# A mixture-of-experts tile loop on VectorE: where the next expert's number is loaded into a register

## The chip, the cores and the metric

The kernel runs on one core of a Trainium2 chip. The metric is the device time of one execution in microseconds. TensorE (PE) multiplies matrices and transposes, ScalarE (ACT), VectorE (DVE) and GpSimd (POOL) compute elementwise, and SyncE (SP) only starts DMAs. Each engine has a sequencer of its own that works through its instructions in order; engines wait for each other through semaphores.

## The reference, cut to what matters

One transformer block over 2048 tokens of width 128, with adaptive layer norm in front of both halves:

```
h = layernorm(x) * (1 + ca) + sa
x = x + ga * attention(h)                     # 16 heads of 64, causal
h = layernorm(x) * (1 + cb) + sb
expert = argmax(h @ Wr.T + br)                # one of 8 experts for each token
y = relu(h @ W1[expert].T + b1[expert]) @ W2[expert].T + b2[expert]
x = x + gb * y
```

The change touches only the last two lines.

## The kernel before, in words

The attention half fills the first 955 us or so. Its order of work on TensorE, ScalarE and VectorE is written out ahead by a planner (`Plan`); the change doesn't touch it.

Then the tokens are sorted by expert. Every token's row is scattered by GpSimd to a place in a table in HBM (`x_sorted`, L557), so that each block of 128 rows belongs to one expert. There are 23 such blocks (`SLOTS`), called tiles below, numbered from 0. `tile_expert` holds in SBUF, as integers, which expert each tile has. All experts' weights lie in SBUF (`experts`), and the four next tiles' own copies of them in `chosen` (`CHOSEN` is 4 places, tile k uses place k % 4). VectorE fills a place by loading the tile's expert number from `tile_expert` into a register (`value_load`, L1067) and copying 1156 columns from an address made with that register (L1068).

For each tile k the engines do this:

- SyncE reads the tile's rows from the sorted table (L525), up to 12 tiles ahead.
- VectorE normalises tile k + 4 (L1086, four tiles ahead: `NORMED` is 4).
- TensorE transposes the normalised tile k + 1 (L724), multiplies tile k with its first weights (`hidden`, L733) and tile k - 2 with its second weights (`output`, L743), in that order. fp32 makes eight matmul instructions of each of the latter two.
- ScalarE scales the transposed tile (L831) and applies bias and relu (L840, four instructions).
- VectorE adds the second bias to the tile's input rows (L1094), waits until TensorE has the tile's result (`y_full`, L1096), for the store of the tile four before (`y_stored`) and for its own sum (L1099), and adds both (L1100), which raises `y_taken`. It waits for `y_taken` (L1104) and copies the weights for tile k + 4 over those of tile k.
- GpSimd waits for `y_taken` and stores the tile's rows to their tokens' places with an indirect DMA (L564).

So TensorE iteration m begins with the transpose of tile m + 1, which needs VectorE's L1086 of tile m + 1, and ends with the result of tile m - 2. VectorE's own order for a tile is L1086, L1094, L1100, L1067, L1068. The copies are made in the tiles 0 to 18; the last four tiles make none. Four copies are made ahead of the loop.

Of the kernel before, what the change touches and what calls it, by code (L numbers as in the profile page):

```python
# [64 lines left out]
class Plan:  # L65
# [8 lines left out]
    def __init__(self):  # L74
# [22 lines left out]
        while any(self.ahead.values()):  # L97
# [4 lines left out]
            if kind is None:  # L102
# [12 lines left out]
                 dve=("norm", "sum", "lo", "add", "resid", "top", "take"))  # L115
# [143 lines left out]

def adaln_block(nc, x, w_qkv, w_out, Wr, br, W1, b1, W2, b2, c_in, wmod, out):  # L260
    _, S, E = x.shape
    _, H, D3 = w_qkv.shape
    D = D3 // 3
    NE, FF, _ = W1.shape
# [7 lines left out]
    SLOTS = T + NE - 1  # L272
    CHOSEN = 4
# [9 lines left out]
    with ExitStack() as ctx:  # L283
        def sb(name, shape, dt=F32):
            return ctx.enter_context(nc.sbuf_tensor(name, shape, dt))
# [85 lines left out]
        tile_expert = sb("tile_expert", [P, SLOTS], I32)  # L371
# [479 lines left out]
        def _(dve):  # L851
# [211 lines left out]
            dve.wait_ge(w2_in, 32)  # L1063
            dve.wait_ge(chosen_known, 1)

            def copy_expert(i, slot_no):
                expert = dve.value_load(tile_expert[0:1, bass.ds(i, 1)], min_val=0, max_val=NE - 1)  # L1067
                dve.tensor_copy(chosen[:, slot_no:slot_no + 1, :],  # L1068
                                experts[:, bass.ds(expert, 1), :]).then_inc(expert_copied, 1)

# [4 lines left out]
                    m = dve.tensor_tensor(w, w, gate_b[:].unsqueeze(1).broadcast_to([P, n, E]), ALU.mult)  # L1075
            link(m)
            for i in range(CHOSEN):
                copy_expert(i, i)

            def normalise_tile(k):  # L1080
                if k >= NORMED:

                    dve.wait_ge(tile_turned, k - NORMED + 1)
                dve.wait_ge(tile_read[k % IN_SLOTS], 16 * (k // IN_SLOTS) + 16)
                row = tile_in[:, k % IN_SLOTS, :]
                dve.tensor_scalar(tile_normal[:, k % NORMED, :], row[:, 0:E], row[:, MEAN:MEAN + 1],  # L1086
                                  row[:, RSTD:RSTD + 1], ALU.subtract, ALU.mult).then_inc(tile_normed, 1)
# [3 lines left out]
            for k in range(SLOTS):  # L1091
                if k + NORMED < SLOTS:
                    normalise_tile(k + NORMED)
                dve.tensor_tensor(tile_x[:, k % 2, :], tile_in[:, k % IN_SLOTS, 0:E],  # L1094
                                  chosen[:, k % CHOSEN, 2 * FF + FT:EXPERT], ALU.add).then_inc(x_summed, 1)
                dve.wait_ge(y_full, k + 1)  # L1096
                if k >= 4:
                    dve.wait_ge(y_stored[k % 4], 16 * (k // 4))
                dve.wait_ge(x_summed, k + 1)  # L1099
                dve.tensor_tensor(tile_y[:, k % 4, :], ps_five[:, 2 + k % 2, 0:E], tile_x[:, k % 2, :],  # L1100
                                  ALU.add).then_inc(y_taken, 1)
                if k + CHOSEN < SLOTS:

                    dve.wait_ge(y_taken, k + 1)  # L1104
                    copy_expert(k + CHOSEN, k % CHOSEN)


# [25 lines left out]
```

## Time and profile before

| | |
|---|---|
| median of 3 runs | 1067.04 us (1066.79 to 1068.41) |
| the profiled execution | 1067.29 us |
| its span from first to last instruction | 1065.5 us |
| PE busy | 999.7 us, 94% |
| DVE busy | 701.0 us, 66% |
| ACT busy | 718.6 us, 67% |
| POOL busy | 43.1 us, 4% |
| granted TensorE clock, mean | 0.98 |

The execution takes 1.8 us more than the span of its instructions. Shares are averages over attention and the tile loop, which have different limits. Names in the rows are those of the buffers in which tiles were placed: `accT` is the normalised tile (L1086) and the biased input (L1094), `v_sb` the finished tile (L1100) and the transposed one (L831), `probs` holds `experts` and `chosen`, `oT` the hidden layer, `hT` the rows as read. DVEq is VectorE's sequencer: instructions there, such as a register load, don't occupy the engine's arithmetic.

### The profile page before, as it was taken

The page shows a single profiled execution, that of the slowest core. Times are in us where ns is not written, and L with a number is a line of the kernel's source. Part 1 is how long each engine was busy: PE and PEld are TensorE (multiplying, and loading weights), DVE is VectorE, ACT ScalarE, POOL GpSimd, SP SyncE. Part 2 cuts the span into 40 slices and gives each one's busy share as a digit, 9 for nine tenths or more (in the row PEclk, how much of TensorE's full clock was granted, in tenths as well). Part 3 has the DMA queues.
Part 4 walks back from the last instruction along what each step waited for, and adds up shares of the span by engine and source line. Part 5 has one row for each costly group of instructions (what it writes and reads, how often), then busy time and mean ns, then how long its engine had stood idle before and what let it go on. Part 6 is the DMA issues. An engine that isn't in the chain of part 4 may idle for free.

```text
span 1065.5 us, 19784 instructions
## 1 busy us (share of the span) xinstructions
PE 999.7 (94%) x7275; PEld 762.3 (72%) x7275; DVE 701.0 (66%) x2234; ACT 718.6 (67%) x1317; POOL 43.1 (4%) x55
## 2 busy tenths in 40 slices
PE   4999999999999999999999999999999999986386
PEld 2677777777777777777777777777777777755376
DVE  4976667856866577666785686657766678555264
ACT  2977767767667677776776776767777677642264
POOL 0000000000000000000000000000000000002444
PEclk9999999999999999999999999999999999996699
DMA  9300020002100020002000210002000100030210
GB/s 202 70 21 1 22 50 21 2 10 48 34 1 2 20 51 21 1 21 50 22 1 19 47 26 1 2 20 51 21 2 21 41 21 1 2 99 16 59 50 17
DMA packets 33199, 31.53 MB, mean 30 GB/s; under 512 B 12181, under 2 KB 22209, under 8 KB 33104
## 3 DMA queue, kind: packets, MB, share of 16 engines
q1 hardware_dynamic: 31856, 28.15, 11.3%
q0 software_dynamic: 1248, 2.13, 0.6%
q8 instruction: 58, 0.95, 0.4%
q14 instruction: 37, 0.30, 0.1%
HBM read 9.83 MB, written 4.12 MB: 13 GB/s over the span
## 4 chain that ended last, share of the span: by engine, by line
PE 85%; DVE 5%; issue 3%; POOL 2%; ACT 1%; DMA 1%; DVEq 1%; SPq 0%; POOLq 0%
PE ps L619 25%; PE ps L656 24%; PE ps L630 22%; PE ps L598 5%; PE ps L639 3%; PE ps L667 3%; PE ps L602 2%; POOL x_sorted L557 1%; DVEq L1067 1%; DVE q_split L926 1%; ACT q_split L791 1%; PE ps L707 1%; PE ps L733 1%; DVE accT L1086 1%; DVE v_sb L1100 1%
## 5 line engine op out<-in xcount | busy, mean ns | idle before, releaser
L619 PE MATMUL ps<-k_split,q_split 128*128 128x512 f32 (+2 forms) x1280 | 370.1, 396 | 4.1 <-DVE q_split L926 2.0
L805 ACT ACTIVATE probs<-probs,neg_max 128x128 f32<-128x128 f32 (+15 forms) x256 | 308.5, 1206 | 41.7 <-DVE neg_max L954 39.4
L947 DVE TENSOR_SCALAR_CACHE_REDUCE probs<-ps 128x512 f32<-128x512 f32 (+1 forms) x384 | 249.6, 667 | 100.0 <-PE ps L630 66.7
L813 ACT COPY pT<-ps 128x512 f32<-128x512 f32 (+1 forms) x435 | 234.2, 564 | 109.7 <-PE ps L630 105.6
L630 PE MATMUL ps<-ident,probs 128*128 128x128 f32 x2176 | 304.4, 273 | 1.4 <-DVE pT L966 1.3
L630 PEld LDWEIGHTS ps<-ident,probs 128*128 128x128 f32 x2176 | 256.0, 140 | 60.7 <-issue 29.4
L656 PE MATMUL ps<-pT,v_sb 128*64 128x256 f32 (+1 forms) x2304 | 272.6, 373 | 0.0
L619 PEld LDWEIGHTS ps<-k_split,q_split 128*128 128x128 f32 x1280 | 201.0, 190 | 48.8 <-issue 28.6
L656 PEld LDWEIGHTS ps<-pT,v_sb 128*64 128x64 f32 x2304 | 152.3, 136 | 87.1 <-issue 26.6
L950 DVE CUSTOM_DVE_ANT_0 probs<-ps,causal 128x256 f32<-128x256 f32 (+3 forms) x256 | 130.9, 511 | 27.6 <-PE ps L619 26.3
L966 DVE COPY pT<-ps 128x512 f32<-128x512 f32 (+1 forms) x141 | 92.3, 659 | 32.9 <-PE ps L630 30.2
L926 DVE SCALAR_TENSOR_TENSOR q_split<-ps,q_split 64x512 fp32r<-64x512 f32 x64 | 44.1, 688 | 60.0 <-ACT q_split L791 58.8
L598 PE MATMUL ps<-hT,w_pair 128*128 128x512 f32 x128 | 63.0, 607 | 0.9 <-ACT hT L777 0.9
L821 ACT COPY rinv_b<-ps 128x256 f32<-128x256 f32 x64 | 23.7, 370 | 49.7 <-PE ps L639 43.9
L557 POOL DMA_INDIRECT x_sorted<-x_sb,slot x16 | 16.5, 1032 | 978.6 <-DVE slot L1052 974.0
L791 ACT ACTIVATE q_split<-ps 64x512 fp32r<-64x512 f32 x64 | 37.8, 590 | 24.8 <-PE ps L598 24.3
L977 DVE TENSOR_TENSOR oT<-ps,rinv_b 128x256 f32<-128x256 f32 x64 | 27.1, 424 | 33.2 <-PE ps L656 32.2
L805 ACT ACTIVATION_READ_ACCUMULATOR probs<-probs,neg_max 128x1 f32 x256 | 48.6, 190 | 0.0
L791 ACT ACTIVATE k_split<-ps 64x512 fp32r<-64x512 f32 x64 | 37.9, 592 | 11.9 <-PE ps L598 11.0
L930 DVE TENSOR_TENSOR k_split<-ps,k_split 64x512 fp32r<-64x512 f32 x64 | 44.0, 688 | 2.9 <-ACT k_split L791 1.7
L954 DVE TENSOR_REDUCE neg_max<-row_max 128x1 f32<-128x1 f32 (+3 forms) x256 | 39.8, 155 | 8.9
L602 PEld LDWEIGHTS ps<-w_pair,hT 128*128 128x128 f32 x256 | 32.8, 192 | 12.3 <-issue 10.3
(126 smaller groups left out, 610.4 us busy)
## 6 DMA issues: line engine op xcount, KB each, us to landing
k_split<-k_split SPq DMA_DIRECT2D x64, 256.0 KB, 3.7
probs<-in_L_ffn_W_dram SPq DMA_DIRECT2D x1, 2048.0 KB, 8.5
w_pair<-in_L_attn_w_qkv_dram SPq DMA_DIRECT2D x24, 64.0 KB, 3.1
hT<-x_sorted SPq DMA_DIRECT2D x23, 65.5 KB, 1.9
x_sorted<-zeros SPq DMA_DIRECT2D x1, 1495.0 KB, 13.8
x_sb<-in_L_attn_x_dram SPq DMA_DIRECT2D x4, 256.0 KB, 5.3
wo_pair<-in_L_attn_w_out_dram SPq DMA_DIRECT2D x8, 64.0 KB, 2.6
probs<-in_L_ffn_b_dram SPq DMA_DIRECT2D x1, 512.0 KB, 9.7
```

What stands on the lines that cost most here:

```text
L598: pe.matmul(ps_ring[:, s.bank, :], w_pair[:, p % 2, j, :], hT[:, c * BANK:(c + 1) * BANK], start=True, stop=True).then_inc(bank_full[s.ban ...
L602: m = pe.matmul(ps_ring[:, s.bank, P * t:P * t + P], hT[:, (TPC * c + t) * P:(TPC * c + t + 1) * P], w_pair[:, p % 2, 2, :], start=True, s ...
L619: m = pe.matmul(ps_ring[:, s.bank, 0:w], q_split[r % 2][:, q0:q0 + P], k_split[r % 2][:, part, k0:k0 + w], start=(part == 0), stop=(part = ...
L630: m = pe.transpose(ps_turn[:, n % TURN_BANKS, P * r:P * r + P], probs[:, g % 2, r, j * P:j * P + P], ident[:])
L656: m = pe.matmul(ps_o[D * h:D * h + D, P * u0:QG], v_sb[:, j, D * h:D * h + D], turned[:, u0:2, h, :], start=(j == 0), stop=(j == 2 * g + 1 ...
L791: m = act.mul(dst[own_half(h), c * BANK:(c + 1) * BANK], ps_ring[own_half(h), bank, :], Q_SCALE if j == 0 else 1.0)
L805: act.activation(row, row, ACT.Exp, bias=neg_max[:, g, r:r + 1], accum_out=row_sum[:, g, r:r + 1]).then_inc(exp_done, 1)
L813: act.copy(pT[:, n % PT_SLOTS, lo:BANK], ps_turn[:, n % TURN_BANKS, lo:BANK]).then_inc(turn_taken[n % TURN_BANKS], 1)
L926: m = dve.scalar_tensor_tensor(out=q_split[h][own_half(1 - h), cols], in0=whole, scalar=Q_SCALE, in1=q_split[h][own_half(h), cols].bitcast ...
L947: dve.tensor_scalar(row, ps_ring[:, bank, 0:w], 1.0, LOWEST, ALU.mult, ALU.max, accum_out=highest).then_inc(bank_free[bank], 1)
L950: dve.tensor_tensor_reduce(row, ps_ring[:, bank, 0:w], causal[:, BANK - w:], 1.0, LOWEST, ALU.add, ALU.max, highest).then_inc(bank_free[ba ...
L966: dve.tensor_copy(pT[:, n % PT_SLOTS, lo:BANK], ps_turn[:, n % TURN_BANKS, lo:BANK]).then_inc(turn_taken[n % TURN_BANKS], 1)
```

## The change

The register load is taken out of the function that copies. In the loop it now stands between the sum of L1094 and the wait for the tile's result; the copy stays behind the wait for `y_taken` and gets the register. The four copies ahead of the loop load and copy in the order of before.

```diff
-            def copy_expert(i, slot_no):
-                expert = dve.value_load(tile_expert[0:1, bass.ds(i, 1)], min_val=0, max_val=NE - 1)
+            def expert_of(k):
+                return dve.value_load(tile_expert[0:1, k:k + 1], min_val=0, max_val=NE - 1)
+
+            def copy_expert(expert, slot_no):
                 dve.tensor_copy(chosen[:, slot_no:slot_no + 1, :],
                                 experts[:, bass.ds(expert, 1), :]).then_inc(expert_copied, 1)
@@
             for i in range(CHOSEN):
-                copy_expert(i, i)
+                copy_expert(expert_of(i), i)
@@
                 dve.tensor_tensor(tile_x[:, k % 2, :], tile_in[:, k % IN_SLOTS, 0:E],
                                   chosen[:, k % CHOSEN, 2 * FF + FT:EXPERT], ALU.add).then_inc(x_summed, 1)
+                following = expert_of(k + CHOSEN) if k + CHOSEN < SLOTS else None
                 dve.wait_ge(y_full, k + 1)
@@
                     dve.wait_ge(y_taken, k + 1)
-                    copy_expert(k + CHOSEN, k % CHOSEN)
+                    copy_expert(following, k % CHOSEN)
```

## Rows read from the trace of the kernel before

**Rows 1.** Stretch, length, busy us of PE, PEld, DVE, ACT, POOL; granted clock.

```profile
1010.54:1052.67 42.13, 36.17 (x291) 32.87 (x289) 26.64 (x70) 27.32 (x87) 18.23 (x18) 1.00 0.15 41
```

**Rows 2.** The chain that ended last, one tile: start us, us, what.

```profile
1022.75 0.33 DVE accT L1086
...
1023.41 0.30 DVE v_sb L1100
...
1023.75 0.30 DVEq L1067
...
1024.08 0.19 DVEq L1067
...
1024.31 0.02 DVEq L1067
...
1024.36 0.06 DVEq L1068
...
1025.21 0.34 DVE accT L1086
```

**Rows 3.** Waits of 1010.5 to 1054.4 us: total us, times, longest us.

```profile
DVE probs L1068 <- DVE v_sb L1100: 13.7, 18, 0.8
...
PE ps L724 <- DVE accT L1086: 5.4, 15, 0.6
```

**Rows 4.** Timeline of VectorE, same tile: start us, us, engine, line, operation.

```profile
1023.00 0.28 DVE L1094 TENSOR_TENSOR accT<-hT,probs 128x128 f32<-128x128 f32 x1
...
1024.46 0.83 DVE L1068 COPY probs<-probs 128x1156 f32 x1 [0.76 <-DVE v_sb L1100]
```

**Rows 5.** Line L1067, whole execution: ns min/median/max, first and last start us.

```profile
L1067 DVEq TENSOR_LOAD <-tile_expert x23: 300/303/618, 986.3 to 1053.7; - x23
```

**Rows 6.** Timeline of VectorE ahead of the loop: two of its four copies.

```profile
987.41 1.52 DVE L1068 COPY probs<-probs 128x1156 f32 x2 [1.11 <-issue]
```

**Rows 7.** Line L1067, 987.42 to 987.5 us: the second load.

```profile
L1067 DVEq TENSOR_LOAD <-tile_expert x1: 310/310/310, 987.4 to 987.4; - x1
```

**Rows 8.** Line L1084, 1023 to 1025 us: the wait ahead of L1086.

```profile
L1084 DVEq EVENT_SEMAPHORE x1: 21/21/21, 1024.5 to 1024.5; - x1
```

**Rows 9.** Line L943, 402.2 to 402.5 us: waits in the attention half.

```profile
L943 DVEq EVENT_SEMAPHORE x2: 21/21/21, 402.3 to 402.4; - x2
```

**Rows 10.** Timeline of VectorE, 402 us: what ran meanwhile.

```profile
402.14 0.69 DVE L966 COPY pT<-ps 128x512 f32<-128x512 f32 x1
...
402.96 0.66 DVE L947 TENSOR_SCALAR_CACHE_REDUCE probs<-ps 128x512 f32<-128x512 f32 x1
```

**Rows 11.** Timeline of TensorE, 1008.6 to 1011 us: one iteration without a wait.

```profile
1008.60 0.27 PE L724 MATMUL ps<-ident,accT 128*128 128x128 f32 x1
...
1009.60 1.06 PE L743 MATMUL ps<-probs,oT 128*128 128x128 f32 x8
1010.94 0.33 PE L724 MATMUL ps<-ident,accT 128*128 128x128 f32 x1 [0.28 <-ACT oT L840]
```

**Rows 12.** The chain that ended last, the loop's end.

```profile
1053.06 0.33 PE ps L724
...
1055.31 1.13 PE ps L733 x8
1056.44 2.69 PE ps L743 x24
...
1059.16 0.30 DVE v_sb L1100
```

**Rows 13.** Timeline of GpSimd, the first tile stored.

```profile
1009.94 1.56 POOL L564 DMA_INDIRECT out_dram<-v_sb,hT  x1 [11.46 <-DVE v_sb L1100]
```

**Rows 14.** Timeline of VectorE at tile 0.

```profile
1009.86 0.76 DVE L1068 COPY probs<-probs 128x1156 f32 x1 [0.77 <-DVE v_sb L1100]
1010.54 0.34 DVE L1086 TENSOR_SCALAR accT<-hT 128x128 f32<-128x128 f32 x1
```

**Rows 15.** Timeline of all engines, GpSimd at tile 6's store.

```profile
1024.50 0.98 POOL L564 DMA_INDIRECT out_dram<-v_sb,hT  x1 [1.48 <-DVE v_sb L1100]
```

## The prediction

> **What bounds the kernel now.** I read the busy time of the tile loop's stretch first. From 1010.54 to 1052.67 us, 42.13 us, no engine is full: TensorE is busy for 36.17 (its ends are modelled and overlap), VectorE for 26.64, ScalarE for 27.32, at a granted clock of 1.00, which is 2.4 GHz [rows 1]. So the limit is a ring of waits, and the chain that ended last shows which. In a middle tile it never leaves VectorE: L1086 at 1022.75, L1094 (not shown), L1100 at 1023.41, then four instructions of VectorE's sequencer in a row, and the copy at 1024.46 [rows 4]; the next L1086 starts at 1025.21 [rows 2]. A tile takes 2.46 us in these rows. Over the loop, from TensorE's transpose at 1010.94 to the one at 1053.06, it is 42.12 / 17 = 2.478 us [rows 11, 12].
>
> The table of waits says the same from both sides. VectorE's arithmetic sat idle 18 times, 13.7 us in all and 0.76 each time, between L1100 and the copy; nobody else is waited for in it. TensorE in turn waited for VectorE's L1086 [rows 3]. VectorE doesn't wait for TensorE's result in the steady loop: L1094, which it needs, runs from 1023.00 to 1023.28 [rows 4], and L1100 starts 0.13 us later [rows 2].
>
> **What the change takes away.** L1100 ends at 1023.71. From there to the copy's start stand the load 0.30, register arithmetic of L1067 0.19, its assertion 0.02, the address arithmetic of L1068 0.06, and gaps of 0.03 to 0.05 around each [rows 2]. The load, its arithmetic and assertion move, and three gaps of 0.03 with them: 1024.36 - 1023.75 = 0.61 us a tile. Address arithmetic and copy stay, so 0.14 us is left between L1100's end and the copy. If the wait for y_taken, which the load carried, becomes an instruction of its own, it costs between 0.02 and 0.09 us more (a wait of 0.02 [rows 8] and up to two gaps of 0.03). No DMA moves; SyncE and GpSimd have the same instructions, but GpSimd's store now meets the copy at another moment (below). The change adds no wait to the engine.
>
> **What it costs in the new place.** The load now stands behind L1094 and ahead of L1100. No row shows a load there, so I bound it.
>
> - The lower end is 0. The sequencer works ahead of the arithmetic. The wait that belongs to L1086 was through at 1024.5 [rows 8], under the copy that ran from 1024.46 for 0.83 us [rows 4], and L1086 itself started at 1025.21. It also hands over whole instructions ahead: two waits of L943 were through at 402.3 and 402.4 [rows 9] while the L966 copy of 402.14 was still at work; between two such waits the code always has a reduction of L947 or L950, and the first of them started at 402.96 [rows 10]. So behind the copy the sequencer hands over L1086 and L1094 and should reach the load about 0.2 us after the copy's start. Load, arithmetic, assertion and gaps, 0.61, then end 0.8 us after the copy's start. L1100 can't start before 1025.21 + 0.66 - 1024.46 = 1.4 us after it, because it waits for L1094's sum. The whole piece is hidden, with 0.6 us to spare.
> - A middle value: the load waits until L1094 has started. L1094 starts at 1023.00, 0.25 behind L1086 [rows 4]. Then load and the rest take 0.63, the satisfied wait and its gap some 0.06, and L1100 starts 0.94 to 0.96 behind L1086 instead of 0.66: 0.29 of the 0.61 is lost.
> - The upper end: the load waits until L1094 has ended (0.54 behind L1086). L1100 then starts about 1.24 behind L1086, a loss of 0.58.
>
> I take 0, because both rows on working ahead are about this sequencer, and one of them in this very place.
>
> The Trainium skill bears on this twice. Its page "Perfetto Trace Analysis", section on the DVE / Act engine instruction, says that the sequencer pushes an instruction into a wait queue and is then ready for the next; by that rule the cost is 0, as in the rows above. "DMA: Bandwidth & Descriptors", section on latency and other measured facts, gives a tensor load a floor of about 600 ns. The trace disagrees: 300 to 303 ns is usual, and only the first of 23 took 618 [rows 5]. By the page's figure the loop's load would still be hidden under the copy, and at the upper end the change would lose.
>
> **What is late next.** VectorE's own ring becomes 0.66 (L1086 to L1100) + 0.29 (L1100) + 0.14 + 0.68 to 0.75 (copy to the next L1086, [rows 14] and [rows 2]) = 1.77 to 1.84 us, with a wait of its own 1.79 to 1.93. That is no longer the limit. TensorE's stream is 17 instructions of about 0.112 (24 in 2.69 us, [rows 12]): L724 at 1008.60, L743 from 1009.60, and eight times 0.112 behind it, so the next L724 could start at 1010.50 and started at 1010.94 [rows 11]. So TensorE's limit is 1.90 us a tile.
>
> The ring through both engines has to be looked at too. TensorE's L724 starts 0.39 behind the start of L1086, its result releases L1100 2.10 later (1008.60 to 1009.60 + 1.06, and 0.04), and L1100 to the L1086 two tiles on is 1.11 to 1.27: 3.60 to 3.76 us for two tiles, 1.80 to 1.88 each. It is under 1.90, by little. ScalarE needs 27.32 / 17 = 1.6 us a tile [rows 1], below it as well. So TensorE binds at 1.90.
>
> **The sum.** (1) The loop's first transpose that waits starts at 1010.50 instead of 1010.94: L1086 moves from 1010.54 to 1009.93, so it isn't what is waited for. 0.44. (2) 17 tiles at 2.478 - 1.90 = 0.578: 9.83. (3) At the end TensorE's L733 of tile 22 started at 1055.31, 2.25 behind the transpose of 1053.06, because the last copy had to end; without that wait it is 1.90: 0.35. What follows, three results in 2.69 us, the last L1100, stores and end, moves as a block [rows 12]. Together 10.6. Three limits lie within 0.1 us of each other, so I expect hand-overs to give some of it back, 0.2. That makes 10.4: 1067.29 - 10.4 = 1056.9 for the profiled execution, which was 0.25 above the median of the runs; against the median 1056.6 us. By itself this case reaches from 1055.6 (nothing given back, a somewhat shorter end) to 1058.3 (VectorE at 1.93 with lost hand-overs).
>
> **The rivals.**
>
> B. The load starts only when L1094 has started. VectorE's ring is 1.77 to 1.93 + 0.29 = 2.06 to 2.22 and binds. 17 tiles give 17 x 0.26 to 0.42 = 4.4 to 7.1, the first L1086 0.6 and the end 0.3: 1059 to 1061.7, about 1060. For it: no load of the trace had a compute instruction ahead of it that hadn't started; the one at 987.4 came with the start of the copy of 987.41 [rows 6, 7]. Against it: that copy had nothing to wait for, so the row is as good for the forecast.
>
> C. The load waits for L1094's end. Then 0.58 of 0.61 comes back ahead of L1100, the ring is 2.35 to 2.5, and the gain is 17 x 0 to 0.12 and up to 0.9 at both ends: 1064 to 1067, about 1065.5. For it: nothing that I found. Against it: the load of 987.4 took its 310 ns while the copy of 987.41 ran, two such copies taking 1.52 us [rows 6, 7].
>
> D, slower. GpSimd's store and VectorE's copy share something. A store begins 0.79 us after L1100's end. Today that is 0.04 after the copy's start (1024.50 and 1024.46): the store takes its plain 0.98 and the copy 0.83 instead of 0.76 [rows 4, 14, 15]. At tile 0 the store came 0.08 after the copy and took 1.56, so it waited until the copy was out of the way [rows 13, 14]. With the copy 0.61 earlier each store falls in the last third of a copy and waits, as at tile 0. If the store, once let in, shuts out L1086, which also reads and writes SBUF, for its 0.95 us, the ring is 1.8 + 0.95 = 2.75 and the kernel is 17 x 0.27 = 4.6 us slower, some 1071.5. The point from which it decides is 0.7 us of blocking. Against it: at tile 0 L1086 started 0.68 behind the copy and took 0.34 while the store ran [rows 14], as everywhere else. Then VectorE loses nothing, and even gains 0.07 on the copy.
>
> The page "SBUF — State Buffer", section on who interferes with whom, says that a VectorE copy in its two-port mode and a GpSimd instruction hold the shared port for a whole instruction, and that whoever issues first blocks the other. Rows 13 and 14 agree for tile 0, where the store waits; at tile 6 both run at once, 35 ns apart, which this rule doesn't have. By it, applied to L1086 as well, D comes out.
>
> E. The change doesn't do what it says: L1067's register arithmetic, 0.19, stays with the copy, or something that no row shows holds the loop at 2.4 us. The first alone gives a ring of 2.0 to 2.15 and a time as in B; the second no change.
>
> **Chances.** Forecast 0.68; B, with the first half of E, 0.14; C 0.08; no change by the second half of E 0.05; D 0.05. What a measurement of this kernel can tell from no change is about 0.2%, 2.1 us. Faster by more than that are the forecast, B and a third of C: 0.85. Within it: the rest of C and E: 0.10. Slower: 0.05. The range takes in the forecast's own and B: 1055.3 to 1061.5; C and D stay out, 0.18.
>
> **What would show it.** In the changed profile the sequencer's TENSOR_LOAD starts 0.1 to 0.3 us after the copy's start and ends before L1086 starts (hidden); in B it starts just behind L1094's start, in C behind its end, and L1100 starts 0.95 or 1.24 behind L1086 instead of 0.66. From L1100's end to the copy it is 0.14 to 0.23. TensorE has no idle time ahead of L724, transposes follow at 1.90, and VectorE's waits turn to TensorE's L743. Stores take up to 1.1 us, and L1086 still 0.34. The forecast is wrong if L1100 moves away from L1086, if L1086 starts more than 0.75 behind the copy, or if TensorE's stream runs above 1.90 a tile for a reason of its own.

## The result and the profile after

| | before | after |
|---|---|---|
| median | 1067.47 us (4 runs, 1066.79 to 1068.41) | 1056.96 us (4 runs, 1055.61 to 1058.02) |
| the profiled execution | 1067.29 us | 1058.02 us |
| its span | 1065.5 us | 1056.2 us |
| transposes of tiles 5 and 22 start at | 1010.94, 1053.06 | 1011.99, 1044.22 |
| a tile of the loop | 2.478 us | 1.896 us |

The changed kernel takes 0.990 of the time before (95% interval 0.9883 to 0.9917). Ahead of the prediction the median before was 1067.04 us, of three executions; a fourth, 1067.9 us, has joined them. One of e8's five executions below, 1074.0 us at a granted clock of 0.94 where its others had 0.99, is left out of the comparisons.

In the changed kernel's code the lines behind the change have moved: the copy is L1070 (was L1068), the wait for a tile read L1086 (L1084), the normalising L1088 (L1086), the sum L1096 (L1094), the wait for it L1102 (L1099), the final add L1103 (L1100). The load is still L1067.

Busy time of the loop's stretch, in the columns of [rows 1]: TensorE now fills it, 34.00 of 34.00 us, as does its weight loading, at a granted clock of 1.00. The ends of matmuls are modelled; the starts further down, 1.90 us apart without a wait, say the same.

```profile
1010.00:1044.00 34.00, 34.00 (x308) 34.00 (x307) 27.05 (x72) 26.78 (x91) 17.09 (x18) 1.00 0.18 50
```

The table of waits over the loop (total us, times, longest) answers [rows 3]. Nobody waits for VectorE's normalising any more, and the wait of 0.76 us between final add and copy is gone from the table: 0.14 us is left of it. VectorE's final add waits for TensorE's L743 instead. The 5.3 us is tile 0, which waits for the loop to fill.

```profile
DVE v_sb L1103 <- PE ps L743: 9.6, 19, 5.3
ACT oT L840 <- PE ps L733: 7.6, 19, 0.4
```

One tile in the timeline of all engines, for [rows 2, 4, 15]: final add at 1019.77, copy at 1020.21, 0.14 us after the add's end, normalising at 1020.88, 0.67 behind the copy. The final add of the next tile, 1021.67, waits 0.24 us for TensorE and so comes 0.79 behind the normalising.

```profile
1019.77 0.29 DVE L1103 TENSOR_TENSOR v_sb<-ps,accT 128x128 f32<-128x128 f32 x1 [0.24 <-PE ps L743]
...
1020.21 0.76 DVE L1070 COPY probs<-probs 128x1156 f32 x1
...
1020.86 0.98 POOL L564 DMA_INDIRECT out_dram<-v_sb,hT  x1 [0.92 <-DVE v_sb L1103]
1020.88 0.34 DVE L1088 TENSOR_SCALAR accT<-hT 128x128 f32<-128x128 f32 x1
1021.14 0.29 DVE L1096 TENSOR_TENSOR accT<-hT,probs 128x128 f32<-128x128 f32 x1
...
1021.67 0.29 DVE L1103 TENSOR_TENSOR v_sb<-ps,accT 128x128 f32<-128x128 f32 x1 [0.24 <-PE ps L743]
```

The load that stands behind the sum of 1021.14 in the program, by its line (count, ns min/median/max, start in us). It starts at 1020.4 under the copy of 1020.21, and its assertion runs at 1021.0 for 23 ns, before that sum has even started.

```profile
L1067 DVEq TENSOR_LOAD <-tile_expert x1: 383/383/383, 1020.4 to 1020.4; - x1
L1067 DVEq FUSED_REGOPS  x1: 190/190/190, 1020.8 to 1020.8; - x1
L1067 DVEq SEQ_ASSERT  x1: 23/23/23, 1021.0 to 1021.0; - x1
```

TensorE's timeline at the start of the loop, for [rows 11]: transpose, eight and eight matmuls, and the next transpose 1.90 us after the one before, with no wait.

```profile
1010.09 0.27 PE L724 MATMUL ps<-ident,accT 128*128 128x128 f32 x1
1010.20 1.06 PE L733 MATMUL ps<-v_sb,probs 128*128 128x128 f32 x8
1011.10 1.06 PE L743 MATMUL ps<-probs,oT 128*128 128x128 f32 x8
1011.99 0.27 PE L724 MATMUL ps<-ident,accT 128*128 128x128 f32 x1
```

And the end of the chain that ended last, for [rows 12]: L733 of tile 22 follows TensorE's own work at once.

```profile
1045.38 0.89 PE ps L743 x8
1046.28 0.89 PE ps L733 x8
1047.17 2.69 PE ps L743 x24
```

### The profile page after: what moved, and what is told of

Read it like the earlier page. It is cut to its first block, busy times and chain, and to the rows that moved or that the text cites. A ratio compares the mean times of both kernels' runs of the same rounds, so it can differ in the third digit from the quotient of the medians.

```text
span 1056.2 us, 19784 instructions
## 1 busy us (share of the span) xinstructions
PE 996.4 (94%) x7275; PEld 763.0 (72%) x7275; DVE 700.1 (66%) x2234; ACT 716.9 (68%) x1317; POOL 42.6 (4%) x55
## 3 DMA queue, kind: packets, MB, share of 16 engines
HBM read 9.83 MB, written 4.12 MB: 13 GB/s over the span
## 4 chain that ended last, share of the span: by engine, by line
PE 88%; DVE 4%; issue 2%; DMA 2%; POOL 2%; ACT 1%; SPq 0%; POOLq 0%; DVEq 0%
PE ps L619 25%; PE ps L656 23%; PE ps L630 22%; PE ps L598 5%; PE ps L639 3%; PE ps L602 3%; PE ps L667 3%; PE ps L733 2%; PE ps L743 2%; POOL x_sorted L557 2%; DMA k_split<-k_split 1%; DVE q_split L926 1%; ACT q_split L791 1%; PE ps L707 1%; DMA probs<-in_L_wmod_dram 0%
## 5 line engine op out<-in xcount | busy, mean ns | idle before, releaser
L557 POOL DMA_INDIRECT x_sorted<-x_sb,slot x16 | 17.4, 1090 | 978.4 <-DVE slot L1052 973.9
```

## The experiments

Two readings were open after the comparison. Theory: the load is free in its new place because VectorE's sequencer works ahead, and TensorE's stream of 1.90 us a tile is the new limit. Rival: the load itself matters little, and the gain came from the copy moving 0.6 us away from the start of GpSimd's store (the copy did fall from 0.83 to 0.76 us). For each kernel the time of a tile is read from TensorE's transposes of tiles 5 and 22, (second - first) / 17. Each ratio is against executions of the kernel before that were made alongside (medians 1067.26 us for e1 to e4, 1068.44 for e5 to e8, 1067.20 for e9 to e11), so the ratios can be compared between rows more closely than the medians.

| kernel | median us | ratio to before (95%) | transposes 5, 22 at | us a tile |
|---|---|---|---|---|
| before | 1067.47 | | 1010.94, 1053.06 | 2.478 |
| after | 1056.96 | 0.990 (0.9883 to 0.9917) | 1011.99, 1044.22 | 1.896 |
| e1, two loads | 1059.21 | 0.9923 (0.9905 to 0.9941) | 1011.60, 1045.21 | 1.977 |
| e2, three loads | 1068.59 | 1.0013 (1.0004 to 1.0023) | 1008.71, 1052.62 | 2.583 |
| e3, load after the sum | 1066.92 | 0.9996 (0.9984 to 1.0009) | 1011.97, 1053.15 | 2.422 |
| e4, load beside the add | 1060.21 | 0.9937 (0.9919 to 0.9954) | 1010.11, 1046.42 | 2.136 |
| e5, before, half the second matmuls | 1066.51 (one run) | | 1010.55, 1052.73 | 2.481 |
| e6, after, half the second matmuls | 1057.34 (one run) | | 1012.41, 1042.75 | 1.785 |
| e7, no load | 1057.04 | 0.9895 (0.9877 to 0.9913) | 1010.00, 1042.23 | 1.896 |

In the kernel before and in e1 to e6 one or two of these tiles are longer than the rest by 0.08 to 0.37 us. In the kernel before it is one: the copy of 1037.17 started 1.13 us after the arithmetic's last work instead of 0.76. The sequencer pauses there between two of its instructions, and the cause is open. The means in the table include these tiles.

```profile
1037.17 0.77 DVE L1068 COPY probs<-probs 128x1156 f32 x1 [1.13 <-issue]
```

**e1 and e2: the load done twice, three times.**

```diff
                 following = expert_of(k + CHOSEN) if k + CHOSEN < SLOTS else None
+                for extra in range(1):            # e2: range(2)
+                    if k + CHOSEN < SLOTS:
+                        expert_of(k + CHOSEN)
```

> The changed kernel with each loop load done twice (the second one's register isn't used). Theory (the sequencer works ahead, a load is free while it ends before L1094's sum does; TensorE binds at 1.90 us a tile): one load with its arithmetic ended 0.84 us after the copy's start in the changed profile, a second one adds 0.61 to 0.69 and ends at 1.45 to 1.53, and the final add could start at 1.35. So VectorE's ring is 1.92 to 2.03 us against TensorE's 1.90: the tile takes 1.9 to 2.05 us and the time is 0.4 to 2.5 us above the changed kernel's 1057. Rival (the gain came from the copy meeting GpSimd's store at another moment, not from the load): the copy starts as soon as in the changed kernel, so 1.90 a tile and no change.

> The same with each loop load done three times. Theory: the third one is beyond any cover and adds its whole 0.61 to 0.69 us: 2.5 to 2.7 us a tile, 17 x 0.6 to 0.8 = 10 to 14 us above the changed kernel, at or above the kernel before, 1067 to 1071. Rival (copy and store): 1.90 a tile, 1057.

Measured: 1.977 and 2.583 us a tile, as the theory has it; the rival's 1.90 fails both times. The times, 1059.21 and 1068.59 us, lie in the ranges expected. The timeline of VectorE in e1 shows two loads at the edge of their cover. The final add (L1106 here) of 1023.66 follows the sum's start by 0.56, and that of 1025.65 by 0.61:

```profile
1023.10 0.29 DVE L1096 TENSOR_TENSOR accT<-hT,probs 128x128 f32<-128x128 f32 x1
1023.66 0.29 DVE L1106 TENSOR_TENSOR v_sb<-ps,accT 128x128 f32<-128x128 f32 x1 [0.28 <-DVE accT L1096]
...
1025.04 0.28 DVE L1096 TENSOR_TENSOR accT<-hT,probs 128x128 f32<-128x128 f32 x1
1025.65 0.29 DVE L1106 TENSOR_TENSOR v_sb<-ps,accT 128x128 f32<-128x128 f32 x1 [0.33 <-PE ps L743]
```

In the chain of e1 the second of these ends with the sequencer's own work: the second load's arithmetic and assertion are through at 1025.50, then come the wait and the add. The releaser named behind that add, L743, isn't what it waited for longest; the chain names the sequencer.

```profile
1024.92 0.31 DVEq L1067
...
1025.48 0.02 DVEq L1067
...
1025.55 0.05 DVEq L1105
...
1025.65 0.30 DVE v_sb L1106
```

In e2 the final add of most tiles is 1.17 to 1.20 behind the sum's start (1021.10 to 1022.27). The next tile is one of two that paused as well, 1.53 (1023.64 to 1025.17).

```profile
1021.10 0.28 DVE L1096 TENSOR_TENSOR accT<-hT,probs 128x128 f32<-128x128 f32 x1
1022.27 0.29 DVE L1106 TENSOR_TENSOR v_sb<-ps,accT 128x128 f32<-128x128 f32 x1 [0.89 <-DVE accT L1096]
...
1023.64 0.28 DVE L1096 TENSOR_TENSOR accT<-hT,probs 128x128 f32<-128x128 f32 x1
1025.17 0.29 DVE L1106 TENSOR_TENSOR v_sb<-ps,accT 128x128 f32<-128x128 f32 x1 [1.24 <-issue]
```

The third load adds 0.61 us a tile, all of it. The kernel is slower than before, by little: 2.583 is more than 2.478, and the ratio of the times is 1.0013 with an interval just above 1.

**e3: the load behind the wait for the sum.**

```diff
-                following = expert_of(k + CHOSEN) if k + CHOSEN < SLOTS else None
                 dve.wait_ge(y_full, k + 1)
                 if k >= 4:
                     dve.wait_ge(y_stored[k % 4], 16 * (k // 4))
                 dve.wait_ge(x_summed, k + 1)
+                following = expert_of(k + CHOSEN) if k + CHOSEN < SLOTS else None
```

> The changed kernel with the load behind the wait for L1094's sum instead of ahead of it, still ahead of the final add; the copy follows the final add as closely as in the changed kernel. Theory: nothing covers the load any more, the final add starts 0.58 to 0.65 us later, VectorE's ring is 0.67 + 0.6 + 0.29 + 0.14 + 0.68 = 2.38 us and binds; 17 x 0.48 = 8 us above the changed kernel, 1065. Rival (copy and store): as the changed kernel, 1057.

2.422 us a tile where about 2.38 was expected, a time of 1066.92 us where 1065 was, and no gain over before that can be measured. The copy is where the changed kernel has it, 0.44 behind the final add, and takes 0.76; 0.06 us a tile is all that this leaves. So the copy's place isn't the cause, the load's cover is. The timeline shows both, 1.05 from sum to add and 0.44 from add to copy:

```profile
1023.85 0.29 DVE L1096 TENSOR_TENSOR accT<-hT,probs 128x128 f32<-128x128 f32 x1
1024.90 0.29 DVE L1103 TENSOR_TENSOR v_sb<-ps,accT 128x128 f32<-128x128 f32 x1 [0.77 <-DVE accT L1096]
1025.34 0.76 DVE L1070 COPY probs<-probs 128x1156 f32 x1
```

This is also what rival C of the prediction described, built: it had said a ring of 2.35 to 2.5.

**e4: the load between the final add and the wait for y_taken.**

```diff
-                following = expert_of(k + CHOSEN) if k + CHOSEN < SLOTS else None
                 dve.wait_ge(y_full, k + 1)
@@
                 if k + CHOSEN < SLOTS:
+                    following = expert_of(k + CHOSEN)
                     dve.wait_ge(y_taken, k + 1)
```

> The kernel before with the load between the final add and the wait for y_taken, so only ahead of that one wait. Theory: the load starts about 0.04 us after the start of the final add (0.29 us) and is covered by it alone; copy 0.83 us behind the add's start against 0.43 in the changed kernel and 1.05 in the one before; ring 1.78 + 0.40 = 2.18 us; 17 x 0.28 = 5 us above the changed kernel, 1062. If a load has to wait for the end of a running instruction instead: 2.4 us a tile, 1066 to 1067.

2.136 against 2.18 expected, and 1060.21 us against 1062; copy 0.76 behind the add's start (1023.00 to 1023.76), where 0.83 was expected. Here the load didn't wait for the end of the running add. Moving it past only the one wait gives 0.34 of the loop's 0.58 us.

```profile
1023.00 0.29 DVE L1102 TENSOR_TENSOR v_sb<-ps,accT 128x128 f32<-128x128 f32 x1
1023.76 0.76 DVE L1070 COPY probs<-probs 128x1156 f32 x1 [0.47 <-DVE v_sb L1102]
```

**e5 and e6: TensorE made shorter, before and after.** Both leave out half of the second layer's matmuls.

```diff
-                for f in range(FT):
+                for f in range(2):
                     m = pe.matmul(ps_five[:, 2 + k % 2, 0:E], hidT[:, k % 4, f, :],
...
-                        stop=(f == FT - 1))
+                        stop=(f == 1))
```

> The kernel before with half of TensorE's second matmuls left out (two of the four 128-row pieces of each tile's second layer, so its output is a partial sum). Theory (VectorE's ring binds before the change): TensorE's stream falls from 1.90 to 1.45 us a tile, and the tile still takes 2.47 us; only the end is shorter, by some 1 us. If TensorE had a share in the old ring, the tile gets shorter.

> The changed kernel with the same half of the second matmuls left out. Theory: TensorE's 1.90 no longer binds, and VectorE's ring shows, 0.67 + 0.29 + 0.14 + 0.68 = 1.78 us a tile. ScalarE's 1.6 stays below it. If something else held the changed kernel at 1.90 (the stores, ScalarE), the tile stays at 1.90.

Before, 0.45 us less of TensorE's work a tile changes nothing: 2.481 for 2.478, and TensorE's wait ahead of the transpose only grows from 0.34 to 0.79 (tile 22, before and e5):

```profile
1053.06 0.33 PE L724 MATMUL ps<-ident,accT 128*128 128x128 f32 x1 [0.34 <-DVE accT L1086]
1052.73 0.33 PE L724 MATMUL ps<-ident,accT 128*128 128x128 f32 x1 [0.79 <-DVE accT L1086]
```

After, the same cut takes 0.11, down to 1.785, and the chain is all VectorE's: copy, the load under it, sum, add. So the changed loop has VectorE's ring 0.11 us below TensorE's stream, and neither stores nor ScalarE hold it at 1.90. The span is 1054.1 us for 1056.2; the single time, 1057.34, doesn't show it, since more lay outside the span in that execution (3.2 us for 1.8).

```profile
1022.12 0.34 DVEq L1067
...
1022.50 0.19 DVEq L1067
1022.69 0.06 DVE accT L1088
...
1022.89 0.30 DVE accT L1096
...
1023.31 0.29 DVE v_sb L1103
```

**e7: no load at all.**

```diff
-                expert = dve.value_load(tile_expert[0:1, bass.ds(i, 1)], min_val=0, max_val=NE - 1)
                 dve.tensor_copy(chosen[:, slot_no:slot_no + 1, :],
-                                experts[:, bass.ds(expert, 1), :]).then_inc(expert_copied, 1)
+                                experts[:, i % NE:i % NE + 1, :]).then_inc(expert_copied, 1)
```

> The kernel before without any register load: the copies take a place known when the program is built, so the weights are those of a wrong expert and the output differs. Theory: nothing is left to win over the changed kernel, whose load is free already; TensorE binds, 1.90 us a tile, the changed kernel's time within 0.2%. If the early load still costs something, this is faster than the changed kernel.

1.896 a tile and 0.9895, as the changed kernel (1.896, 0.990): nothing that can be measured is left of the load's cost.

**e8 to e11: the start of the loop.** The times of the profiles above differ by a start that shows no relation to the edits: tile 4's transpose began at 1008.60 before and 1010.09 after, and between 1006.81 (e2) and 1010.70 (e6) in the others. Two things in it looked removable: scatters of GpSimd that ran beside VectorE's work took up to 1.56 us instead of 0.96, and TensorE ran at 1.2 GHz at first. Two edits to the changed kernel, in four kernels (the declaration of the semaphore `gated` isn't shown):

```diff
@@ ScalarE
+            act.wait_ge(chosen_known, 1)
+            act.wait_ge(gated, 1)
+            for i in range(CHOSEN):
+                expert = act.value_load(tile_expert[0:1, i:i + 1], min_val=0, max_val=NE - 1)
+                act.copy(chosen[:, i:i + 1, :], experts[:, bass.ds(expert, 1), :]).then_inc(expert_copied, 1)
@@ VectorE
-            link(m)
-            for i in range(CHOSEN):
-                copy_expert(expert_of(i), i)
+            m.then_inc(gated, 1)
+            dve.wait_ge(expert_copied, CHOSEN)
@@ TensorE
+            for i in range(27):                   # e8: range(22)
+                pe.matmul(ps_o[:], ident[:], oT[:, 0:BANK], start=True, stop=True)
             turn_tile(0)
```

> The changed kernel with two additions meant to start the loop sooner. ScalarE instead of VectorE loads and makes the four copies ahead of the loop, and TensorE runs 22 matmuls of 128x512 into an unused PSUM bank while it waits for the first tile. In the changed profile four of GpSimd's 16 scatter instructions took 1.3 to 1.56 us instead of 0.96 beside VectorE's work, 1.9 us in all, and TensorE's clock was 1.2 GHz for the first 6 us of the loop. Expected: the copies' part of the scatter time, about 1.2 us, and 2 to 3 us of the slow clock come back: 1053 to 1054. If neither is on the path, 1057. If the added matmuls last too long, the first transpose waits for them and the time is above 1057.

> The changed kernel with only the four copies ahead of the loop given to ScalarE, with their loads. With them and the added matmuls together the profile showed scatters of 1.50, 1.50 and 1.91 us beside VectorE's multiplications with the gate instead of beside the copies. If the collisions only move with the phase of the two engines, the scatter's 16 instructions sum to 16.5 to 18 us as in the changed kernel (17.4) and the time stays within 0.1% of 1057. If the copies were their main cause, 16.2 to 16.6 and 1055.5 to 1056.5.

> The changed kernel with 27 matmuls of 128x512 into an unused PSUM bank in TensorE's idle time ahead of the loop. 22 of them took 19.05 us, ended 5.8 us before the first transpose, and the loop still began at 1.2 GHz; 27 should take 23.4 us and end within 1.5 us of it. If the clock then stays at 2.4 GHz, TensorE's matmuls start 0.11 us apart from the loop's first tile on instead of 0.21 over the first 24 or so, 2 to 3 us earlier in all: 1054 to 1055. If the clock falls all the same, 1057; if the last added matmuls hold the first transpose back, up to 1 us is lost again.

> Both additions, the copies on ScalarE and the 27 matmuls. If each gives what is hoped, 1053 to 1054; if only the clock does, 1054 to 1055; if the scatter ends sooner than the added matmuls, those bind and it is no better than with the matmuls alone.

| kernel | median us | ratio to before (95%) | scatter, 16 in us | transposes 0 and 4 at |
|---|---|---|---|---|
| after | 1056.96 | 0.990 (0.9883 to 0.9917) | 17.4 | 1002.76, 1010.09 |
| e8, copies on ScalarE and 22 matmuls | 1056.98 | 0.9888 (0.987 to 0.9907) | 17.7 | 1004.89, 1012.36 |
| e9, copies on ScalarE | 1054.51 | 0.9892 (0.9875 to 0.9908) | 15.8 | 998.99, 1005.79 |
| e10, 27 matmuls | 1055.37 | 0.9893 (0.9877 to 0.9908) | 16.5 | 1001.23, 1006.74 |
| e11, both | 1053.58 | 0.9875 (0.986 to 0.989) | 15.7 | 1000.03, 1005.48 |

Three of the four missed what was hoped for. e8 was to reach 1053 to 1054 us and stayed at 1057; e9 came out below its 1055.5 to 1056.5 and its scatter below 16.2 us; e10 just above 1055. e11 lies within 1053 to 1054.

In e8 the 22 matmuls ended 5.8 us before the first transpose, and the clock was low again: 0.50 from 1005 to 1010 us, which is 1.2 GHz. In e10 27 of them end where the transpose starts, and the clock stays at 1.00, 2.4 GHz. In e11, with the copies on ScalarE as in e8, it stays at 1.00 too. Busy time rows of e8 and e10, then e10's timeline of TensorE:

```profile
1005.00:1010.00 5.00, 4.86 (x21) 4.34 (x22) 1.48 (x5) 2.41 (x8) 0.00 (x0) 0.50 0.51 120
```

```profile
1000.00:1005.00 5.00, 4.12 (x24) 2.65 (x23) 1.93 (x6) 2.61 (x9) 0.00 (x0) 1.00 0.58 136
```

```profile
977.79 23.34 PE L749 MATMUL ps<-oT,ident 128*128 128x512 f32 x54
1001.23 0.33 PE L724 MATMUL ps<-ident,accT 128*128 128x128 f32 x1
```

From tile 0's transpose to tile 4's it is 7.33 us after and 5.51 in e10, 1.8 us less. e9's scatter is shorter, 15.8 for 17.4 us, but e8's isn't with the same copies on ScalarE: there VectorE's multiplications with the gate met the scatters instead. So the copies' share isn't settled by one profile each. By the ratios none of e8, e9 and e10 is clear of the changed kernel. e11, 1053.58, is the fastest of all here, but its interval and the changed kernel's overlap between 0.9883 and 0.989.

## Why the prediction was right

It said 1056.6, the measured median is 1056.96. The mechanism and its terms hold; that the time agrees within 0.4 us is partly luck, because the medians carry a start of the loop that no term covers: tile 4's transpose began anywhere from 1006.81 to 1010.70 us in the profiles of e1 to e7. By its steps, in the profiled executions:

- The first waiting transpose: 0.44 forecast. Tile 5's follows tile 4's by 1.90 instead of 2.34: 0.44.
- 17 tiles: 9.83 forecast. 42.12 - 32.23 = 9.89. Some 0.3 of it isn't the load but the one longer tile of the kernel before, which the prediction's 2.478 had averaged in; the tile of its rows took 2.46.
- The end: 0.35 forecast. From tile 22's transpose to the last 24 matmuls it is 1047.17 - 1044.22 = 2.95, before 1056.44 - 1053.06 = 3.38: 0.43. Of it 0.35 lies ahead of L733, as forecast.
- Given back in hand-overs: 0.2 forecast, none found. The three sum to 10.76 us. The profiled execution after took 9.27 less than the one before because its loop also began 1.49 us later: 10.76 - 1.49 = 9.27. About half of it, 0.73, is there at tile 0's transpose (1002.76 for 1002.03), with a longer scatter ahead of it (17.4 for 16.5 us); the other 0.76 comes between the transposes of tiles 0 and 4 (7.33 for 6.57), where the clock was low for longer (0.61 granted from 1005 to 1010 us, 0.89 before). e1 to e7 show such starts in either direction without relation to the edit. The medians differ by 10.51.
- The load's cost of 0, the choice on which all hung: shown by the load's rows and by e1, e2, e3 and e7. It starts 0.17 us after the copy (0.2 forecast) and the piece ends 0.84 after it (0.8). It isn't quite as short as before: its median is 373 ns where it was 303. In that tile it had 0.5 us to spare, not 0.6: with no wait for TensorE the final add comes 1.35 behind the copy (1023.31 and 1021.96 in e6).
- The wait for y_taken became no instruction of its own. The address arithmetic carries it, and add's end to copy is 0.14, the lower value.
- TensorE's 1.90 as the new limit: 1.896 a tile, and VectorE's ring of 1.77 to 1.84 behind it: 1.785 in e6. The middle ring of 1.80 to 1.88 through both engines left no mark.
- Rivals B and C failed: the load starts 0.7 us ahead of the sum that they had it wait for, or wait out. With them goes the first half of E, since 0.14 is left ahead of the copy; the second half goes with the 1.90 that was reached.
- Rival D failed: L1088 takes 341 to 348 ns in all 23 tiles, and GpSimd's store isn't in the chain before the last tile.
- One sign of being wrong was badly put. The final add did move away from the normalising, from 0.66 to 0.79, and the forecast holds all the same: the add waits for TensorE's result, not for the load. In e6, where TensorE is shorter, it is 0.68 (1022.63 to 1023.31).

One step was wrong without effect. The prediction said that each store, falling in the last third of a copy, would wait for it as at tile 0 (1.56 us, [rows 13]), up to 1.1 us. It didn't wait: 980 ns in the median and 995 at most, by the store's line. The part of the store that a copy holds back doesn't begin at once, and by then the copy is over (last section).

```profile
L564 POOL DMA_INDIRECT out_dram<-v_sb,hT x23: 980/980/995, 1011.4 to 1051.8; - x23
```

## What to carry to other kernels

Read the sequencer's rows between two waits: a register load there cost 0.6 us here with its arithmetic, though no engine is shown as busy. Put it where the instructions handed over ahead of it keep the engine busy for longer than the load takes, and ahead of the wait that ends the cover. Behind that wait it was paid in full: 2.422 us a tile in e3, where VectorE's ring without that cost is 1.785 (e6). Then add up each engine's stream, because the gain ends at the next one. VectorE's ring fell by 0.69 us, 0.61 for the load and 0.07 for the shorter copy; the tile gained 0.58, since TensorE's 1.90 lies just above VectorE's 1.78.

## What the runs showed that I had not expected

- A store doesn't wait for a copy from its own start on. In the kernel before, e4 and e3, stores that began 0.08, 0.33 and 0.57 us into a copy of 0.76 took 1.56, 1.29 and 1.04 us instead of 0.98, and each ended 0.84 to 0.88 us after the copy's end. So some 0.10 to 0.14 us of the store had gone by beside the copy, an estimate from these rows and [rows 13, 14]; a store at 0.65 gets to the part that waits at 0.75 to 0.79, as the copy ends. That fits the medians by the store's line, 980 ns in the changed kernel and 1295 ns in e4.

```profile
1023.76 0.76 DVE L1070 COPY probs<-probs 128x1156 f32 x1 [0.47 <-DVE v_sb L1102]
...
1024.09 1.29 POOL L564 DMA_INDIRECT out_dram<-v_sb,hT  x1 [0.82 <-DVE v_sb L1102]
```

```profile
1037.54 0.77 DVE L1070 COPY probs<-probs 128x1156 f32 x1 [0.22 <-DVE v_sb L1103]
...
1038.11 1.04 POOL L564 DMA_INDIRECT out_dram<-v_sb,hT  x1 [1.44 <-DVE v_sb L1103]
```

- One that started 0.04 us after a copy's start ran beside it while the copy took 0.83 [rows 4, 15]; why it wasn't held is open. The page "SBUF — State Buffer" of the Trainium skill, section on who interferes with whom, has whole instructions block each other. The three stores above agree but for their first tenth of a microsecond; the one at 0.04 doesn't.
- The register load took longer in its new place: in the loop 301 to 448 ns, median 374, where it was 300 to 315, median 303. What lengthens it was not tried.

```profile
L1067 DVEq TENSOR_LOAD <-tile_expert x18: 301/374/448, 1010.9 to 1043.1; - x18
```

- Matmuls whose results nobody reads, put in TensorE's idle time, kept its clock at 2.4 GHz into the loop when they ran up to it (e10 and e11, 1.00 granted), and not when they ended 5.8 us earlier (e8, 0.50), in one profile each.
